# One unit of four pt_lo to VectorE, two of four w_lo to GpSimd, and one transfer in place of two for narrow attention units

## What is computed

```
xn = layernorm(x)
q, k, v = xn @ Wq.T, xn @ Wk.T, xn @ Wv.T     # 32 query heads, 8 key/value heads, head size 128
q, k = rmsnorm(q, q_norm_w), rmsnorm(k, k_norm_w)
scores = q k^T / sqrt(128) + alibi bias, masked to the past
s = (softmax(scores) @ v) @ Wo.T
g = silu(ffn(xn))                              # a small mixture of 8 low-rank experts
y = x + s * g
```

## Time and profile before

| what | value |
|---|---|
| time, median of 3 runs | 741.79 us |
| lowest and highest | 741.38 and 743.2 us |
| profiled execution | 743.02 us, its span 741.2 us |
| TensorE matmul busy | 720.8 us, 97% |
| VectorE busy | 600.6 us, 81% |
| ScalarE busy | 559.7 us, 76% |
| GpSimd busy | 335.6 us, 45% |
| TensorE's granted clock | 0.998 of full speed |

### The profile page before, as it was taken

One profiled execution on the slowest core, in us unless ns is written; L12 is line 12 of the kernel. 1 busy time (PEld: TensorE's weight loads), 2 busy tenths in 40 slices (PEclk: granted clock), 3 DMA queues, 4 the chain that ended last, 5 costly groups with the idle time before them and its releaser, 6 DMA issues.

```text
span 741.2 us, 14630 instructions
## 1 busy us (share of the span) xinstructions
PE 720.8 (97%) x3741; PEld 605.4 (82%) x3741; DVE 600.6 (81%) x1490; ACT 559.7 (76%) x1440; POOL 335.6 (45%) x320
## 2 busy tenths in 40 slices
PE   8899999999999999999999999999999999999997
PEld 7787878878788888888888888888888887888776
DVE  6857798678886889787986889777986979878985
ACT  4566888587877877777886978778887768769873
POOL 4223434454434543545444543346326434445556
PEclk9999999999999999999999999999999999999999
DMA  8015968687685778868686786958787785867761
GB/s 304 1 30 140 274 170 235 194 239 224 172 267 160 223 203 229 242 158 254 183 231 198 229 241 173 280 141 232 214 229 217 191 264 147 232 196 204 205 191 72
DMA packets 214773, 148.02 MB, mean 200 GB/s; under 512 B 48992, under 2 KB 205536, under 8 KB 214624
## 3 DMA queue, kind: packets, MB, share of 16 engines
q1 hardware_dynamic: 184224, 130.39, 60.7%
q10 hardware_dynamic: 30528, 17.38, 8.9%
HBM read 85.84 MB, written 61.87 MB: 199 GB/s over the span
## 4 chain that ended last, share of the span: by engine, by line
PE 62%; DMA 10%; DVE 9%; issue 7%; ACT 6%; SPq 2%; POOL 2%; ACTq 1%; DVEq 0%; POOLq 0%
PE out_ps L1363 6%; PE qkv_ps L1363 5%; PE out_ps L1365 5%; PE qkv_ps L1364 5%; PE out_ps L1364 5%; PE qkv_ps L1365 5%; DMA x_sb<-turning 5%; PE score_ps L1363 4%; PE score_ps L1365 3%; PE score_ps L1364 3%; PE mix_ps L1363 3%; PE mix_ps L1365 3%; PE mix_ps L1364 3%; DMA turning<-squared 3%; PE turn_ps L1364 2%
## 5 line engine op out<-in xcount | busy, mean ns | idle before, releaser
L589 POOL TENSOR_TENSOR pt_lo<-x_sb,pt_hi 128x512 fp32r<-128x512 f32 x129 | 164.2, 1296 | 257.5 <-ACT pt_hi L795 257.5
L720 ACT ACTIVATE probs<-probs,neg_max 128x128 f32<-128x128 f32 (+3 forms) x256 | 142.1, 559 | 33.3 <-DVE neg_max L1018 32.1
L1018 DVE CUSTOM_DVE_ANT_0 probs<-score_ps,cst,slope 128x128 f32<-128x128 f32 (+3 forms) x256 | 131.0, 543 | 20.0 <-PE score_ps L1365 19.1
L728 ACT ACTIVATE probs<-probs,recip 128x128 f32<-128x128 f32 (+3 forms) x252 | 126.1, 549 | 8.0 <-DVE recip L1025 8.0
L795 ACT ACTIVATE pt_hi<-x_sb 128x512 fp32r<-128x512 f32 x153 | 86.6, 623 | 50.6 <-issue 31.7
L1363 PE MATMUL qkv_ps<-w_hi,xt_hi 128*128 128x256 f32 (+1 forms) x364 | 118.8, 326 | 2.4 <-DVE xt_lo L961 1.5
L1364 PE MATMUL qkv_ps<-w_lo,xt_hi 128*128 128x256 f32 (+1 forms) x364 | 118.4, 325 | 0.0
L1365 PE MATMUL qkv_ps<-w_hi,xt_lo 128*128 128x256 f32 (+1 forms) x364 | 118.0, 324 | 0.0
L1363 PE MATMUL out_ps<-wo_hi,o_hi 128*128 128x512 f32 x252 | 102.5, 407 | 0.8 <-DVE o_lo L1063 0.6
L1039 DVE STREAM_TRANSPOSE squared<-probs 128x256 f32<-128x256 f32 (+3 forms) x124 | 100.4, 810 | 0.1
L579 POOL TENSOR_TENSOR inv_rms<-sums,minus_half 128x5 f32<-128x5 f32 x64 | 76.9, 1202 | 50.1 <-DVE sums L1077 50.1
(11 more groups left out here) (203 smaller groups left out, 1630.3 us busy)
## 6 DMA issues: line engine op xcount, KB each, us to landing
qk_moved<-turning_qk SPq DMA_DIRECT2D x60, 320.0 KB, 3.4
turning_qk<-qk_squared ACTq DMA_DIRECT2D x212, 80.0 KB, 2.2
turning<-squared SPq DMA_DIRECT2D x120, 128.0 KB, 2.4
x_sb<-turning SPq DMA_DIRECT2D x30, 512.0 KB, 5.2
w_raw<-wqkv SPq DMA_DIRECT2D x32, 384.0 KB, 5.0
turning<-squared SPq DMA_DIRECT2D x120, 96.0 KB, 2.1
x_sb<-turning SPq DMA_DIRECT2D x30, 384.0 KB, 4.2
turning<-squared SPq DMA_DIRECT2D x128, 64.0 KB, 2.0
```

Of the source, the lines that this page charges most:

```text
L589: nc.gpsimd.tensor_tensor(by_quad(pt_lo, j), moved_block(t, j), by_quad(pt_hi, j).bitcast(F32), ALU.subtract).then_inc(pt_lo_by_pool, 1)
L720: nc.scalar.activation(probs[:, h, 0:n], probs[:, h, 0:n], ACT.Exp, bias=neg_max[:, h:h + 1], scale=-1.0, accum_out=total[:, h:h + 1]).the ...
L728: nc.scalar.activation(to[:, h, 0:n], probs[:, h, 0:n], ACT.Copy, scale=recip[:, h:h + 1]).then_inc(probs_ready, 1)
L1018: nc.vector.tensor_tensor_reduce(probs[:, h, 0:n], score_bank(t, h), cst[:, C_DIST + SEQ - n:C_DIST + SEQ], slope[:, h:h + 1], HUGE, ALU.a ...
```

## The change

Three things are done. (1) `BY_POOL` goes from 1 to 0, so that VectorE makes all four `pt_lo` of unit 3, and `W_DVE` from 3 to 2, so that GpSimd makes `w_lo` of chunks 2 and 3; in the W slot VectorE makes its two chunks together, and `turned_qk_lo` goes ahead of both `square_probs`. (2) `project_new` takes chunks 0 to 2 through all their products, and chunk 3 afterwards. (3) For narrow units `squared` is laid out so that both pairs of heads stand in one run; one set of four transfers writes them, after both are there, and one transfer reads them. In the opening, in slot 2, `turned_qk_lo` goes ahead of the first `square_probs`.

```diff
-BY_POOL = 1
+BY_POOL = 0
-W_DVE = 3
+W_DVE = 2
...
+WRITTEN = counter([16 * QUADS] * BLOCKS), counter([0, 0, 16 * QUADS, 16 * QUADS] * BATCH)
+MOVED = counter([16, 16, 32, 32] * BATCH)
...
         def moved_block(t, j):
+            if keys_of(t) <= 2:
+                return moved_whole(t).rearrange("p q (s n) -> p q s n", s=2)[:, :, :, j * P // 2:(j + 1) * P // 2]
             return moved[t % 2][:, :, :, j * P // 2:(j + 1) * P // 2]
...
+                if keys_of(t) <= 2:
+                    if soon and u is not None:
+                        sp.wait_ge(qk_lo_ready, K_AND_Q_LO(g, u, 0))
+                        read_qk(g, u)
+                    write_all_probs(g, t)
+                    if u is not None and not soon:
+                        read_qk(g, u)
+                    sp.wait_ge(probs_written[0], WRITTEN[0](g, t, 16 * QUADS))
+                    sp.dma_start(moved_whole(t), turning[t % 2, :, :, 0:2 * n].rearrange("q p n -> p q n")).then_inc(probs_moved, 16)
+                    return
...
+            def write_all_probs(g, t):
+                n = keys_of(t) * P
+                sp.wait_ge(probs_squared, TWO(g, t, 2))
+                for q in range(QUADS):
+                    sp.dma_start(turning[t % 2, q, :, 0:n].rearrange("(k r) n -> r k n", k=QUADS),
+                                 squared_whole[q * QUAD:(q + 1) * QUAD, :, 0:n]).then_inc(probs_written[0], 16)
...
             def slot(g, t, left):
-                if t % BLOCKS == W_SLOT and here(t + 3, left):
+                if t % BLOCKS == W_SLOT:
                     turned_lo(g, t - 2)
...
-                elif t % BLOCKS == W_SLOT:
-
-                    turned_lo(g, t - 2)
...
                 moved_lo(g, t - 2)
-                split_w(g + 1, range(0, W_DVE - 1))
+                split_w(g + 1, range(0, W_DVE))
                 normalize_k(g, t + 2)
                 reciprocals(g, t, 0)
                 reciprocals(g, t, 2)
-                split_w(g + 1, range(W_DVE - 1, W_DVE))
                 normalize_q(g, t + 2)
                 square_both(g, t + 2)
+                turned_qk_lo(g, t + 1)
                 square_probs(g, t, 0)
-                turned_qk_lo(g, t + 1)
                 square_probs(g, t, 2)
...
+                if t == 2:
+
+                    turned_qk_lo(g, t + 1)
                 if here(t, left):
                     square_probs(g, t, 0)
-                if here(t + 1, left):
+                if here(t + 1, left) and t > 2:
                     turned_qk_lo(g, t + 1)
...
+                first, last = range(0, KC - 1), range(KC - 1, KC)
+                for chunks in (first, last):
+                    for to, cols, _ in parts:
+                        if chunks is first and to is parts[1][0]:
+                            pe.wait_ge(k_norm_ready, ONE(g, t - 1, 1))
+                            pe.wait_ge(v_lo_ready, ONE(g, t - 1, 1))
+                        for c in chunks:
                             pe.wait_ge(w_hi_done, (g + t // BLOCKS) * KC + (c + 1))
-                        pe.matmul(to, xt_hi[:, c, rows], w_hi[:, c, cols], start=c == 0, stop=False)
-                        pe.matmul(to, xt_lo[:, c, rows], w_hi[:, c, cols], start=False, stop=False)
...
+                            pe.matmul(to, xt_hi[:, c, rows], w_hi[:, c, cols], start=c == 0, stop=False)
+                            pe.matmul(to, xt_lo[:, c, rows], w_hi[:, c, cols], start=False, stop=False)
+                    for c in chunks:
+                        if c < W_DVE:
+                            pe.wait_ge(w_lo_by_dve, (g + t // BLOCKS - 1) * W_DVE + (c + 1))
+                        else:
+                            pe.wait_ge(w_lo_by_pool, (g + t // BLOCKS - 1) * (KC - W_DVE) + (c - W_DVE + 1))
```

More of the change, by code:

```diff
@@ L125 @@
 PER_BATCH = counter(([1] + [0] * (QB - 1)) * BATCH)
-WRITTEN = counter([16 * QUADS] * BLOCKS)
-MOVED = counter([32] * BLOCKS)
+WRITTEN = counter([16 * QUADS] * BLOCKS), counter([0, 0, 16 * QUADS, 16 * QUADS] * BATCH)
+MOVED = counter([16, 16, 32, 32] * BATCH)
 QK_WRITTEN = counter([16 * QUADS] * BLOCKS)
@@ L172, in build @@
         squared = sb("squared", [QUADS, 2, QB * HPG // 2 * QUAD])
+        squared_whole = squared[:, :, :, :].rearrange("p k s n -> p k (s n)")
         turning = nc.dram_tensor("turning", (2, QUADS, P, SEQ), F32, kind="Internal").ap()
@@ L411, in last_turns, with moved_whole @@
             return sum(keys_of(u) for u in range(BY_PE, t))
+        def moved_whole(t):
+            return moved[t % 2].rearrange("p q s n -> p q (s n)")[:, :, 0:keys_of(t) * P]
         def moved_block(t, j):
+            if keys_of(t) <= 2:
+                return moved_whole(t).rearrange("p q (s n) -> p q s n", s=2)[:, :, :, j * P // 2:(j + 1) * P // 2]
             return moved[t % 2][:, :, :, j * P // 2:(j + 1) * P // 2]
@@ L468, in move @@
                                      qk_squared[q * QUAD:(q + 1) * QUAD, :, :]).then_inc(qk_written, 16)
+                if keys_of(t) <= 2:
[8 more added lines that the diff above has]
+                    return
                 write_probs(g, t, 0)
-                if soon:
+                if soon and u is not None:
                     sp.wait_ge(qk_lo_ready, K_AND_Q_LO(g, u, 0))
@@ L476, in move @@
                 for pair in range(2):
-                    sp.wait_ge(probs_written[pair], WRITTEN(g, t, 16 * QUADS))
+                    sp.wait_ge(probs_written[pair], WRITTEN[pair](g, t, 16 * QUADS))
                     sp.dma_start(to[:, :, pair, 0:n],
                                  turning[t % 2, :, :, pair * n:(pair + 1) * n].rearrange("q p n -> p q n")).then_inc(probs_moved, 16)
+            def write_all_probs(g, t):
[4 more added lines that the diff above has]
+                                 squared_whole[q * QUAD:(q + 1) * QUAD, :, 0:n]).then_inc(probs_written[0], 16)
             def write_probs(g, t, pair):
@@ L789, in moved_hi @@
             def moved_hi(g, t):
-                act.wait_ge(probs_moved, MOVED(g, t, 32))
+                act.wait_ge(probs_moved, MOVED(g, t + 1, 0))
                 if t > 0:
@@ L846, in end @@
                 for pair in range(2):
-                    act.wait_ge(probs_written[pair], WRITTEN(g, before, 0))
+                    act.wait_ge(probs_written[pair], WRITTEN[pair](g, before, 0))
                 normalize_probs(g, before, range(0, 2), late_probs)
@@ L1031, in square_probs @@
                 if t > 0:
-                    dve.wait_ge(probs_written[h // 2], WRITTEN(g, t, 0))
+                    dve.wait_ge(probs_written[h // 2], WRITTEN[h // 2](g, t, 0))
                 if t >= 2 and h == 2:
@@ L1037, in square_probs @@
                         dve.wait_ge(moved_lo_by_dve, DVE_BLOCKS(g, t - 1, 0))
-                blocks = squared[:, :, h // 2, :].rearrange("p k (j h n) -> p h j k n", j=QB, h=HPG // 2)
-                nc.vector.transpose(blocks[:, :, 0:keys_of(t), :, :],
+                if keys_of(t) <= 2:
+                    part = squared_whole[:, :, h // 2 * n // 2:(h // 2 + 1) * n // 2]
+                else:
+                    part = squared[:, :, h // 2, 0:n // 2]
+                nc.vector.transpose(part.rearrange("p k (j h n) -> p h j k n", j=keys_of(t), h=HPG // 2),
                                     probs[:, h:h + 2, 0:n].rearrange("p h (j k n) -> p h j k n", k=QUADS, n=QUAD)).then_inc(probs_squared, 1)
@@ L1408, in project_new @@
                 rows = slice(m * P, (m + 1) * P)
[L1409 to L1415, removed]
-                            pe.wait_ge(w_hi_done, (g + t // BLOCKS) * KC + (c + 1))
-                        pe.matmul(to, xt_hi[:, c, rows], w_hi[:, c, cols], start=c == 0, stop=False)
-                        pe.matmul(to, xt_lo[:, c, rows], w_hi[:, c, cols], start=False, stop=False)
@@ L1419, in project_new @@
[L1419 to L1427, removed]
+                parts = ((q_ps(t), slice(0, QW), q_ready), (qkv_ps[:, 1, 0:QKV - QW], slice(QW, QKV), kv_ready))
@@ new lines, in project_new @@
+                first, last = range(0, KC - 1), range(KC - 1, KC)
[5 more added lines that the diff above has]
+                        for c in chunks:
+                            pe.wait_ge(w_hi_done, (g + t // BLOCKS) * KC + (c + 1))
+                            pe.matmul(to, xt_hi[:, c, rows], w_hi[:, c, cols], start=c == 0, stop=False)
[3 more added lines that the diff above has]
+                            pe.wait_ge(w_lo_by_dve, (g + t // BLOCKS - 1) * W_DVE + (c + 1))
+                        else:
+                            pe.wait_ge(w_lo_by_pool, (g + t // BLOCKS - 1) * (KC - W_DVE) + (c - W_DVE + 1))
+                        for to, cols, done in parts:
+                            product = pe.matmul(to, xt_hi[:, c, rows], w_lo[:, c, cols], start=False, stop=c == KC - 1)
+                            if c == KC - 1:
+                                product.then_inc(done, 1)
```

## The result

The changed kernel takes 750.2 us (median of 4 runs, 748.3 to 752.18) where the kernel before takes 741.59 in the same session: ratio 1.0119, 95% interval 1.0096 to 1.0142. It is slower, as forecast, but by 8.6 us and not by 4.75; the time lies 0.7 us above the range. The profiled execution took 750.36 us, its span 748.5.

What follows compares the result with a forecast made beforehand. TensorE, busy 97%, was taken to be held by VectorE's first-head bias once per group. +5.4 (seven slots) - 0.35 (last group) - 0.3 (opening) = +4.75 on the median 741.79: 746.5 us, range 739.5 to 749.5.

Steps and rivals of the forecast that it cites:

- The lock: VectorE instructions with two SBUF operands block beside GpSimd's SBUF reads, ending 0.55 to 0.56 us after GpSimd's.
- the new B: Start of VectorE's first-head bias of unit 6, where the next group's weights are split: forecast D + 10.69 us.
- D: In that slot, when VectorE ends unit 5's biases and starts the first pt_lo; 183.22 in the second one shown.
- The old B - D: Kernel before, first pt_lo to that bias, seven slots: taken as 9.00 to 10.64 us from the shown profile.
- +5.4: Summed delay in us of the bias over seven weight-splitting slots, new minus old, 0.05 to 1.69 each.
- The opening: Merged read waited for, k_lo of unit 3 ahead of a pair of probs: net -0.3 us taken.
- Merged transfers elsewhere: Narrow units' merged writes and read: up to 1.6 us later but hidden; 0 taken, bounds -1 and +3.
- The last group: VectorE makes the first pt_lo, done at 701.29 in place of GpSimd's 701.64: -0.35 us.
- TensorE's new order: Projection with chunk 3 last: the w_hi wait goes but the bias covers it, gain 0; uncovered, 2.9 us.
- No block: Rival: q_lo isn't held up, bias 0.39 us earlier in each of seven slots, 738.4 us; chance 0.18.
- Compensated: Rival: x_sb arrives late as in the seventh slot, so little is lost, 742.5 us; chance 0.14.
- Merged reads too late: Rival: ScalarE finds two-block units' data missing 14 to 15 times, +3, 749.5 us; chance 0.10.

Runs made afterwards that it cites:

- probs_factor: Changed kernel with the first pair of probs ahead of q_lo and k_lo and the copy of factor done one slot later: ratio 1.0045 to before.
- factor_late: Changed kernel with three w_lo on VectorE, one on GpSimd, and the copy of factor done one slot later: 743.8 us, ratio 1.0030 to before.
- before_again: Kernel before, unchanged, run once more for a second profile: ratio 0.9978, profiled execution 740.48 us.
- order_alone: Kernel before with only TensorE's new order in the projection of unit 8 (new project_new): 740.85 us, ratio 0.9995.
- merge_alone: Kernel before with only the merged writing and reading of narrow units: 741.85 us, ratio 1.0021.
- w_alone: Kernel before with only the edits of the W slot and the last group's pt_lo: 748.41 us, ratio 1.0098.
- three_by_vector: Changed kernel with W_DVE 3 in place of 2, so three w_lo on VectorE and one on GpSimd: 749.6 us, ratio 1.0116 to before.

## Why the prediction was right in kind and wrong in size

- **The lock, and the new B.** Right. Forecast D + 10.69, measured D + 10.42 to 10.66. probs_factor and factor_late, which change what is blocked, moved B by about what the same working gives (10.02 for 10.0, 9.79 for 9.9).
- **The old B - D: the step that failed.** "New minus old, in order: ... sum +5.4" took the old values from one execution of 743.02 us and added the result to a median of 741.79. In that execution x_sb was late in five of the seven W slots, and lateness that the new form swallows was in the old values. Over the four profiles with the old W slot (the shown one, before_again, order_alone, merge_alone) the mean is 9.88, 9.24, 9.55 and 9.71, together 9.60; the new mean is 10.58, so seven slots cost 7 x 0.98 = 6.9. TensorE's stretch of the seven slots gives a little more: 601.2 to 604.8 us in those four, mean 602.6, and 608.9 and 610.7 in w_alone and the changed kernel, 7.2 more on the mean. The term of +5.4 was too small by 1.5 to 1.8 us. The trace had shown a slot where nothing was late (the fifth, 9.00), and seven times 10.69 - 9.00 = 11.8 was the upper bound that the range left out: it took "2 us either way".
- **The opening: mis-sized as much, and in sign.** Forecast -0.3; it is a loss of 1.3 by the two groups of profiles, a miss of 1.6. The reason is the one that the prediction named ("the same read is waited for"): ScalarE's wait there grew by 1.8 us on the mean. The prediction set it off against the moved k_lo, without a row for either, and took the gain for the larger.
- **Merged transfers elsewhere.** Forecast 0, and no run shows anything else. With the opening the two comparisons give 0.16 and 0.21%, 1.2 and 1.5 us, neither clear of zero by the times alone.
- **The last group.** Forecast -0.35. From the scores of unit 5 to those of unit 6 the last group took 7.95 us before and 7.60 after, the forecast 0.35. But it doesn't reach the end: from the scores of unit 5 to the end of the span it is 44.5 in both, and over the four old profiles and the two new ones 44.6 and 44.5. The gain is worth 0.1.
- **TensorE's new order.** Forecast 0, measured 0.9995 (0.9975 to 1.0015): no gain or loss that can be told from zero.
- **The rivals.** No block is refuted by every trace. Compensated looked at arrivals of x_sb later than those shown; the runs had earlier ones, which is the other side. Merged reads too late gave nearly the right time, 749.5, by a mechanism that did not happen: narrow units of the loop don't wait.

The sum with the terms as the profiles give them is 6.9 to 7.2 for the W slots, 1.3 for the opening and -0.1 for the last group: 8.1 to 8.4, where 4.75 was forecast and 8.6 measured, known to 1.7 either way. That the time came out only 0.7 above the range is no sign that the terms were near: both large ones were too small, and the range's upper end had come from a rival that did not happen.

## What to carry to other kernels

When work moves to GpSimd, ask what VectorE has in its list at those microseconds, not how long each engine is busy: here a VectorE instruction with two operands in SBUF, or a copy, that started beside GpSimd's subtraction stood until that had ended, and all that was queued behind it too. A norm out of PSUM (0.67), a transposition (0.84) and an addition with PSUM (0.64) took their usual time beside it. A lock that is taken away may uncover the next one right behind it, so look at every short instruction up to the one that is waited for. And where the old path hangs on an arrival and the new one on a fixed length, the old value of a single profile is a sample: take the slot in which nothing was late as a bound, and keep the sum and the execution that it is added to the same.

## What the runs showed of the hardware

A copy of 128x5, 0.14 us long, took 1.02 us against a GpSimd subtraction of 128x512, and ended 0.03 us after it. Where this one small instruction stands in the list was worth 6.4 us over seven slots (three_by_vector against factor_late); whether GpSimd or VectorE makes a w_lo of 128x768 was worth nothing that can be told (1.0119 and 1.0116) while it stood there. The other unexpected number is how far the arrivals of the same transfers differ between executions of one kernel: ScalarE's waits for x_sb ahead of the W slots were 5.4 us in all in one and 1.9 in another, and the executions took 743.02 and 740.48.
